# A vision tower on one core: local attention with scores on half the rows, scaling on GpSimd, one maximum and one copy per chunk, and the output product inside the loop

## What is computed

```python
h = tokens(x) @ W
h = h + L0_attn(layernorm(h))      # local attention, 16 query heads, one key/value head
h = h + L0_ffn(layernorm(h))       # 8 experts, top 2
h = h + L1_attn(layernorm(h))      # full attention, then batch norm
h = h + L1_ffn(layernorm(h))       # 8 experts, top 1 with capacity
```

```python
mask = (cols <= rows) & (rows - cols <= 128)
scores = einsum('bqgtd,bqgsd->bqgts', q, k) / 8
p = softmax(where(mask, scores, -1e30))
out = einsum(p, v) @ wo.T
```

## Time and profile before

| what | value |
|---|---|
| median of 3 runs | 1309.26 us (1307.86 to 1312.95) |
| the profiled execution | 1307.1 us, of which the span of the trace is 1305.3 us |
| PE busy | 901.9 us, 69% of the span |
| DVE busy | 834.4 us, 64% |
| ACT busy | 481.7 us, 37% |
| POOL busy | 159.6 us, 12% |
| mean granted clock of TensorE | 0.861 of full speed |
| windowed, second image | 374.8 to 499.6 us |
| its PE, DVE, ACT, POOL busy, 374.8 to 491.0 us | 105.75, 91.08, 80.25, 0.00 us |

### The profile page before, as it was taken

One profiled execution on the slowest core, in us unless ns is written; L12 is line 12 of the kernel. 1 busy time (PEld: TensorE's weight loads), 2 busy tenths in 40 slices (PEclk: granted clock), 3 DMA queues, 4 the chain that ended last, 5 costly groups with the idle time before them and its releaser, 6 DMA issues. The chain is left out here.

```text
span 1305.3 us, 18986 instructions
## 1 busy us (share of the span) xinstructions
PE 901.9 (69%) x6390; PEld 564.4 (43%) x6398; DVE 834.4 (64%) x2339; ACT 481.7 (37%) x1687; POOL 159.6 (12%) x116
## 2 busy tenths in 40 slices
PE   4477997775879986766699867766999679320630
PEld 4133664454336654453266534622666347120530
DVE  1387886754778867546788756467988465560235
ACT  0024774142237751321377622312777223000100
POOL 0051000000420000003300000024000000007145
PEclk9888999897879997887899978978999789755775
DMA  7033000000330000002400000014100000300112
GB/s 242 11 62 130 2 2 1 1 1 3 60 132 2 2 2 1 1 3 44 148 2 2 2 1 0 3 27 119 46 2 1 1 1 1 98 1 26 62 47 43
DMA packets 51381, 43.40 MB, mean 33 GB/s; under 512 B 46452, under 2 KB 47892, under 8 KB 50356
## 3 DMA queue, kind: packets, MB, share of 16 engines
q1 hardware_dynamic: 49222, 39.91, 10.5%
q0 software_dynamic: 2048, 2.10, 0.7%
HBM read 29.21 MB, written 4.72 MB: 26 GB/s over the span
## 5 line engine op out<-in xcount | busy, mean ns | idle before, releaser
L696 ACT ACTIVATE work<-ps,small,rq 128x160 f32<-128x160 f32 x512 | 241.3, 481 | 134.5 <-DVE small L659 134.5
L593 PE MATMUL ps<-kT,big 128*128 128x320 f32 x512 | 185.6, 469 | 0.0
L654 DVE TENSOR_REDUCE small<-ps 128x2 f32<-128x320 f32 x256 | 113.7, 486 | 50.3 <-PE ps L593 48.1
L260 PE MATMUL ps<-xT,s_proj_w 64*128 64x512 f32 x384 | 126.6, 794 | 26.1 <-DVE xb L533 13.8
L668 DVE TENSOR_SCALAR work<-work,small 128x128 f32<-128x128 f32 x512 | 112.0, 282 | 4.5
L624 PE MATMUL ps<-turned,vwin 128*64 128x128 f32 x1024 | 84.2, 283 | 27.7 <-ACT big L711 23.7
L696 ACT ACTIVATION_READ_ACCUMULATOR work<-ps,small,rq 128x1 f32 x512 | 101.8, 199 | 0.0
L593 PEld LDWEIGHTS ps<-kT,big 128*128 128x128 f32 x512 | 82.3, 199 | 24.8 <-issue 24.8
L678 DVE COPY turned<-ps 128x512 f32<-128x512 f32 x128 | 87.6, 684 | 2.4 <-PE ps L605 2.4
L260 PEld LDWEIGHTS ps<-xT,s_proj_w 64*128 64x128 f32 x384 | 46.8, 247 | 89.9 <-issue 61.3
L564 POOL TENSOR_TENSOR big<-xb 128x1024 f32<-128x1024 f32 x32 | 75.6, 2374 | 60.0 <-DVE xb L533 60.0
(11 more groups left out here) (240 smaller groups left out, 1504.1 us busy)
## 6 DMA issues: line engine op xcount, KB each, us to landing
xb<-in_x SPq DMA_DIRECT2D x5, 4096.0 KB, 13.5
vrem<-xb SPq DMA_DIRECT2D x64, 64.0 KB, 2.1
s_proj_w<-in_proj_w SPq DMA_DIRECT2D x1, 1536.0 KB, 6.2
sent_rows<-zeros SPq DMA_DIRECT2D x8, 160.0 KB, 4.0
big<-sent_rows SPq DMA_DIRECT2D x5, 256.0 KB, 3.5
answered_rows<-big SPq DMA_DIRECT2D x8, 160.0 KB, 1.8
xb<-in_ffn_w SPq DMA_DIRECT2D x1, 1028.0 KB, 5.5
out<-vrem SPq DMA_DIRECT2D x8, 128.0 KB, 2.0
```

What stands on the lines that cost most here:

```text
L260: ins = nc.tensor.matmul(bank[banks + w][:], proj_w[half_rows(w), cols], xT[half_rows(w), :], start=True, stop=True)
L593: ins = nc.tensor.matmul(tiles, qT[:, c, 4 * hh:4 * hh + 4, :].rearrange("p a t -> p (a t)"), kT[:, :, CHUNK * c:CHUNK * c + SPAN], start= ...
L654: ins = v.tensor_reduce(small[:, c % 4, 0, 2 * e:2 * e + 2], s_bank(c, e)[:, 0:2 * SPAN].rearrange("p (a k) -> p a k", a=2), X, ALU.max)
L696: nc.scalar.activation(probs[:, c % 3, q, :], s_bank(c, q // 2)[:, SPAN * (q % 2):SPAN * (q % 2) + SPAN], ACT.Exp, bias=small[:, c % 4, 1, ...
```

## The change

Seven things are changed together in `windowed`, with what they need in `setup` and `project`:

1. `kT` holds the keys once. The scores of `e` = 0 use partitions 0 to 63 and those of `e` = 1 partitions 64 to 127: four matmuls of 160 columns on half the rows in place of two of 320 on all rows, and the mask matmuls likewise (two per chunk, as before). `e` = 0 and `e` = 1 go to different banks. The groups are ordered q = 2e + hh in place of 2hh + e.
2. One `TENSOR_REDUCE` of 640 columns over both banks, which writes its four maxima to PSUM (`row_max`).
3. The scaling moves from DVE to POOL: two `TENSOR_TENSOR`, of 512 and of 128 columns. DVE keeps the reciprocal and signals `sums_inverted`.
4. The transposes go to bank 4 and the start of bank 5, one set in place of two; one copy of 640 columns by DVE takes both to `pT`, and ACT's `pTr` copy goes away.
5. The values' outputs move from the scores' banks to banks 6 and 7, one set; ACT takes both with one copy of 256 columns, which signals `oT_ready`. `values` is done one step earlier: PE's step n is `scores(n)`, `turn(n-2)`, `values(n-3)`. The `oT` copy of ACT stays at n-4, behind the exponentials of n. `values(c)` now waits for `oT_ready` to reach c, which is the copy of chunk c-1.
6. The output product is made per tile of 128 tokens, 8 matmuls of 64 columns each: seven tiles inside the loop, in `turn` of every fourth chunk from chunk 7 on, and the last after it. DVE adds each to `h` in `add_out`. The product at the end, ACT's copy of it and its transposes go away.
7. `project` writes `kT` with one instruction. `setup` loads the mask and the row selector twice, once per half of the partitions.

```diff
-                        for e in range(2):
-                            r = half_rows(e)
-                            ins = v.scalar_tensor_tensor(out=kT[r, e, WINDOW:], in0=k_turned[r, :], scalar=wqk[r, 0:1],
-                                                         in1=ps[r, 6:8, :].rearrange("p a n -> p (a n)"), op0=ALU.mult,
-                                                         op1=ALU.mult)
-                        ins.then_inc(S["v_dve"], 1)
+                        v.scalar_tensor_tensor(out=kT[:, WINDOW:], in0=k_turned, scalar=wqk[:, 0:1], in1=both_banks(6),
+                                               op0=ALU.mult, op1=ALU.mult).then_inc(S["v_dve"], 1)
...
+                    for hh in range(2):
+                        for e in range(2):
+                            ins = nc.tensor.matmul(tiles[e][:, hh, :],
+                                                   qT[half_rows(e), c, 4 * hh:4 * hh + 4, :].rearrange("p a t -> p (a t)"),
+                                                   kT[half_rows(e), CHUNK * c:CHUNK * c + SPAN], start=False, stop=True,
+                                                   skip_group_check=True)
...
+                def out_product(i):
+                    pe.wait_ge(S["oT_ready"], NQ * (i + 1))
+                    for p in range(PAIRS):
+                        ins = nc.tensor.matmul(wo_at(i), oT[:, p, P * i:P * i + P], sbuf["wo0"][:, p, :], start=(p == 0),
+                                               stop=(p == PAIRS - 1), skip_group_check=True)
...
                 def turn(c):
                     pe.wait_ge(S["scaled"], c + 1)
-                    if c >= 2:
-                        pe.wait_ge(S["pT_ready"], c - 1)
-                        pe.wait_ge(S["pTr_ready"], c - 1)
+                    if c >= 1:
+                        pe.wait_ge(S["pT_ready"], c)
+                    if added(c):
+                        out_product((c - 7) // 4)
...
                 def values(c):
                     pe.wait_ge(S["pT_ready"], c + 1)
-                    pe.wait_ge(S["pTr_ready"], c + 1)
-                    if c >= 2:
-                        pe.wait_ge(S["oT_ready"], c - 1)
-                    pe.wait_ge(S["exp_done"], NQ * min(c + 3, CHUNKS))
+                    if c >= 1:
+                        pe.wait_ge(S["oT_ready"], c)
...
-                                o = s_bank(c, hh)[D * e:D * e + D, 2 * SPAN:2 * SPAN + P]
+                                o = bank[6 + hh][half_rows(e), 0:P]
...
-                for n in range(CHUNKS + 4):
-                    if n >= 4:
-                        values(n - 4)
+                for n in range(CHUNKS + 3):
                     if n < CHUNKS:
                         scores(n)
                     if 2 <= n < CHUNKS + 2:
                         turn(n - 2)
-                pe.wait_ge(S["oT_ready"], CHUNKS)
...
+                    if n >= 3:
+                        values(n - 3)
+                out_product(TILES - 1).then_inc(S["wo_done"], 1)
                 turn_normed(pe, 1)
...
+                        ch.step(v.tensor_reduce(row_max(c),
+                                                ps[:, s_banks(c), 0:2 * SPAN].rearrange("p e (h k) -> p e h k", h=2), X,
+                                                ALU.max))
...
+                        if added(c):
+                            add_out((c - 7) // 4)
+                        v.tensor_copy(pT[:, c % 2, :],
+                                      ps[:, 4:6, :].rearrange("p a n -> p (a n)")[:, 0:(NQ + 1) * P]).then_inc(
+                                          S["pT_ready"], 1)
...
+            @block.gpsimd
+            def _(g):
+                for c in range(CHUNKS):
+                    g.wait_ge(S["sums_inverted"], c + 1)
+                    if c >= 2:
+                        g.wait_ge(S["transposed"], c - 1)
+                    g.tensor_tensor(probs[:, c % 3, :, 0:P], probs[:, c % 3, :, 0:P], bc(small[:, c % 4, 3, :], P),
+                                    ALU.mult)
+                    g.tensor_tensor(own[:, c % 2, :].rearrange("p (q k) -> p q k", q=NQ), probs[:, c % 3, :, P:SPAN],
+                                    bc(small[:, c % 4, 3, :], CHUNK), ALU.mult).then_inc(S["scaled"], 1)
...
                     c = n - 4
                     if c >= 0:
                         a.wait_ge(S["pv_done"], c + 1)
-                        for hh in range(2):
-                            ins = nc.scalar.activation(
-                                oT[:, 4 * hh:4 * hh + 4, CHUNK * c:CHUNK * (c + 1)],
-                                s_bank(c, hh)[:, 2 * SPAN:2 * SPAN + P].rearrange("p (a t) -> p a t", t=CHUNK),
-                                ACT.Copy)
-                        ins.then_inc(S["oT_ready"], 1)
-                a.wait_ge(S["proj_done"], 1)
-                nc.scalar.activation(tokensT, bank[0][:], ACT.Copy).then_inc(S["v_act"], 1)
+                        nc.scalar.activation(
+                            oT[:, :, CHUNK * c:CHUNK * (c + 1)].rearrange("p (h a) t -> p h a t", h=2),
+                            ps[:, 6:8, 0:P].rearrange("p h (a t) -> p h a t", t=CHUNK),
+                            ACT.Copy).then_inc(S["oT_ready"], 1)
```

More of the change, by code:

```diff
@@ L179, in program @@
         pTr_own = sb("pTr_own", [P, 4, P])
-        pTr, own = pTr_own[:, 0:2, :], pTr_own[:, 2:4, :]
+        own = pTr_own[:, 2:4, :]
         sums_turned = pTr_own[:].rearrange("p a n -> p (a n)")
@@ L298, in _ @@
                     r = slice(D * half, D * half + D)
+                    for dst, src in ((row_of_t_rows, "row_of_t"), (window_mask_rows, "window_mask")):
+                        sp.dma_start(dst[D * half:D * half + CHUNK], inp[src]).then_inc(first_sem, 16)
+                        n += 1
                     for dst, src in ((qn, "q_norm"), (kn, "k_norm"), (bq, "bq1"), (bk, "bk1")):
@@ L334, in _ @@
                 v.tensor_tensor(both_halves[:], ident[:, 0:D], ident[:, D:P], ALU.add)
-                v.tensor_copy(row_of_t[0:CHUNK], sbuf["row_of_t"])
-                v.tensor_copy(window_mask[0:CHUNK], sbuf["window_mask"])
+                for half in range(2):
+                    r = slice(D * half, D * half + CHUNK)
+                    v.tensor_copy(row_of_t[r], row_of_t_rows[r])
+                    v.tensor_copy(window_mask[r], window_mask_rows[r])
                 ch.step(v.tensor_scalar(wqk[:], qn[:], kn[:, 0:1], float(np.sqrt(D)), ALU.mult, ALU.mult))
@@ L567, in windowed @@
         def windowed(block, b):
-            def s_bank(c, half):
-                return bank[2 * (c % 2) + half]
             @block.sync
@@ L575, in _, with s_banks, row_max, added @@
                 sp.wait_ge(S["x_loaded"], 16)
+            def s_banks(c):
+                return slice(2 * (c % 2), 2 * (c % 2) + 2)
+            def row_max(c):
+                return ps[:, s_banks(c), HALF - 2:HALF]
+            def added(c):
+                return c % 4 == 3 and c >= 7
+            def wo_at(i):
+                return bank[5][:, HALF - D * (1 + i % 2):HALF - D * (i % 2)]
             @block.tensor
@@ L596, in scores @@
-                    ins.then_inc(S["scores_done"], 1)
+                    tiles = [bank[2 * (c % 2) + e][:, 0:2 * SPAN].rearrange("p (h k) -> p h k", h=2) for e in range(2)]
+                    for e in range(2):
+                        if c < EARLY:
+                            mask, masked = rows(window_mask[half_rows(e), variant, :], 2), tiles[e]
+                        else:
+                            mask = window_mask[half_rows(e), variant].rearrange("p (g k) -> p g k", k=CHUNK)
+                            mask = mask[:, ::SPAN // CHUNK - 1, :].unsqueeze(1).to_broadcast([D, 2, 2, CHUNK])
+                            masked = tiles[e].rearrange("p h (g k) -> p h g k", k=CHUNK)[:, :, ::SPAN // CHUNK - 1, :]
+                        nc.tensor.matmul(masked, row_of_t[half_rows(e)], mask, start=True, stop=True,
+                                         skip_group_check=True)
@@ L663, in _ @@
                         v.wait_ge(S["exp_done"], NQ * (c + 1))
-                        ch.step(v.reciprocal(small[:, c % 4, 3, :], small[:, c % 4, 2, :]))
-                        if c >= 2:
-                            v.wait_ge(S["transposed"], c - 1)
-                        for q in range(NQ):
-                            v.tensor_scalar(probs[:, c % 3, q, 0:P], probs[:, c % 3, q, 0:P], small[:, c % 4, 3, q:q + 1],
-                                            None, ALU.mult)
-                        v.tensor_tensor(own[:, c % 2, :].rearrange("p (q k) -> p q k", q=NQ), probs[:, c % 3, :, P:SPAN],
-                                        bc(small[:, c % 4, 3, :], CHUNK), ALU.mult).then_inc(S["scaled"], 1)
+                        v.reciprocal(small[:, c % 4, 3, :], small[:, c % 4, 2, :]).then_inc(S["sums_inverted"], 1)
                     c = n - 2
@@ L694, in _ @@
                             a.wait_ge(S["transposed"], c - 2)
[L695 to L706 removed]
```

(7 more changed lines are left out.)

80 lines of the change are left out of this document (23 added, 57 removed).

## The result

The changed kernel takes **1695.76 us** (median of 4 runs, 1688.53 to 1700.01), against 1308.56 for the kernel before in the same session: 1.2949 times as long (95% interval 1.2922 to 1.2977), or 387 us more. The forecast was 1600 with a range of 1535 to 1675. The direction was right, and so was the mechanism up to the clock; the size was too small by 96 us, and the result lies outside the range.

A forecast was written before the change was run, and what follows sets the result against it. PE's throughput bound the loop before; a ring through PE, DVE and ACT would bind it after. 27 x (6.1 - 3.16) less 7 is 72.4 us an image, 291 with four images and setup: 1600 us, range 1535 to 1675.

The forecast's parts named there:

- the ring: Loop: `oT` copy, behind exponentials of n, holds `values(n-3)`, and `scores(n+1)` stands behind them; 5.55 us a turn at full clock.
- six step lengths: In the ring: scores to maximum 1.00, maximum to exponential 1.05, exponentials 1.86, copy 0.38, copy to values 0.26, values 0.96 us.
- first four turns: Filling the pipe: chunk 4's scores start 10.6 us after chunk 0's, before 11.9; -1.3 us an image.
- Rivals 3 and 4: Loop: 3, the ring doesn't close, about 1253 us, chance 0.03; 4, POOL late for the transposes, 1697 us, chance 0.03.
- the price of a low clock in a turn: In the ring at 1.2 GHz: at most a doubling of scores and values, 1.8 us; turn 6.5 to 7.3, estimate 6.9.
- I expect it to go to and fro: PE's clock in the loop: alternates between 2.4 and 1.2 GHz, so a turn of 6.1 us, between 5.55 and 6.9.
- PE's busy time should hardly rise: Whole kernel: a sign of the forecast, PE's total busy time hardly rises; no size given.
- Rival 2: Loop: the same ring, always at 1.2 GHz; 1687 us as a median, chance 0.17.
- the end of the stage, -4.5 us: Behind the loop, scores of chunk 31 to DVE's sum: 14.3 us where 18.8 stood, -4.5 us an image.
- `kT` and setup: `kT` in one instruction: -1.1 us an image; setup's two more DMAs and doubled casts: +1.6 us once.
- The output product at nothing: Every fourth turn of the loop: the output product, 1.8 us, lies in PE's gap of 3.1 us in the ring.

The follow-up runs named there:

- first experiment: The changed kernel with ACT's `oT` copy of chunk n-4 moved ahead of the exponentials of chunk n: 1267.84 us, 0.9692 of the kernel before.
- the wait alone: The kernel before with one condition changed, the values of chunk c waiting for the `oT` copy of chunk c-1: 1868.56 us, one run.
- the products out of the ring: The changed kernel with all eight output products per tile, and DVE's eight sums, made behind the loop: 1700.24 us, one run.
- the kernel with the fill: The changed kernel with 12 unread bfloat16 matmuls of 384 columns in PE's gap in turns without an output product: 1522.5 us, one run.
- the scaling's 36 us: The first experiment with the scaling put back on DVE and POOL's part removed: 1303.4 us, 0.9966 of the kernel before.
- the half rows' 45: The first experiment with the scores computed again on all rows, keys stored twice with zeros: 1313.31 us, 1.0048 of the kernel before.
- the product's -21: The first experiment with the output product made once behind the loop, as in the kernel before: 1247.03 us, 0.9537 of the kernel before.

## Why the prediction was right in kind and wrong in size

**Right: the ring.** Its place (ACT's order of exponentials and copy, wanted by `values(n-3)`), its length at full clock (5.51 worked out and 5.55 taken, 5.30 measured), its idle time (2.81 us behind L722 at full clock), and that nothing else closes it. PE waited there 92 times where some 110 were forecast, since the turns with a product at 1.2 GHz have no gap left. The first experiment shows it by opening the ring, and the wait alone shows it by closing it in the old kernel. Four of the six step lengths came within 0.02 us. The other two were shorter than forecast: scores to maximum (0.88 for 1.00) and the end of the copy to the values (0.14 for 0.26). The first four turns took 10.7 us in two images (107.86 to 118.56) and 11.45 in two, 10.6 forecast. Rivals 3 and 4 fell: no turn ran near 3 us, and POOL's product takes 1.04 us and waits 638 us in all.

**Right: the price of a low clock in a turn.** The forecast was 6.9 for 5.55, 1.35 more; measured were 6.66 for 5.30, 1.36 more.

**Wrong: how often the clock is low.** The step "I expect it to go to and fro", with 6.1 between the two levels, failed. In the first and last image the loop from chunk 4 to chunk 31 took 181.5 us (118.56 to 300.07 in the first), in the other two 179.1 (482.78 to 661.89), 6.68 a turn on average. That is about the turn of 6.66: what the products add, the few turns at a higher clock take back. The forecast's reason for the mix was that the output product in the gap makes the work nearly unbroken, so that the clock should rise there. A turn with one and the turn after it:

```profile
149.50:157.50 8.00, 8.00 (x55) 6.68 (x53) 2.04 (x5) 2.25 (x9) 1.40 (x2) 0.50 0.01 2
157.90:160.90 3.00, 1.09 (x11) 0.68 (x9) 1.79 (x4) 1.49 (x7) 1.36 (x2) 1.00 0.01 3
161.40:177.40 16.00, 11.11 (x84) 7.75 (x86) 3.81 (x8) 4.75 (x19) 2.79 (x4) 0.50 0.00 0
```

PE worked all of the 8 us, at 1.2 GHz. The clock did rise behind it, during the next scores, but then came the next gap (busy 1.09 of 3 us), and it was low again when the values ran. The scores and transposes of one turn were all that had it. The unbroken stretch was not needed for such a rise either: with the products out of the ring the clock rose as often. What makes it rise there no run shows. The sign that PE's busy time should hardly rise failed too: it rose by 210 us. At 6.68 for 6.10, the loops are 62 us above the forecast in 108 turns. This hides a piece of luck. With the mix of the forecast (6.1 lies 0.41 of the way from 5.55 to 6.9) the measured levels 5.30 and 6.66 give 5.86, so the mix by itself is 89 us off, and the ring that was taken 0.25 too long gives 27 back. The Trainium skill (TensorE: Matmul & The Clock Gate, section "HAM oscillation — how this bites in real kernels") describes a loop in which every iteration starts at the low clock. Its loop waits 3 to 5 us in each iteration; here gaps of 2.81 and then 2.25 us did it, and the windows' 0.58 and 0.61 agree with the low clock. Rival 2, which has this as its mechanism, was the nearest of the cases with 1687, though it had a chance of only 0.17. Its nearness is partly luck: 24 us too much for the loops (404 for 380) stand against 39 too little for all the rest.

**Wrong: the end of the stage, -4.5 us.** From the scores of chunk 31 to DVE's sum it took 22.8 us (300.07 to 322.67 and 0.2 for the sum), where 18.8 stood before and 14.3 was forecast. The steps named in the forecast add up to 13.3 (3.9, 1.6, three times 1.8, 0.4 for the copy, 1.8 and 0.2), so 1.0 of its 14.3 has no step. Two rows of the changed kernel, and one of the kernel with the fill:

```profile
309.67 3.68 PE L615 MATMUL ps<-s_wo,big 128*128 128x64 f32 x16
...
322.67 0.22 DVE L662 TENSOR_TENSOR h<-h,ps 128x64 f32<-128x64 f32 x1 [7.26 <-PE ps L615]
```

```profile
277.04 0.22 DVE L668 TENSOR_TENSOR h<-h,ps 128x64 f32<-128x64 f32 x1 [4.14 <-PE ps L615]
```

At full clock the same end took 14.9 us (262.35 to 277.04 and 0.2). The forecast had the end at 2.4 GHz while it let the loop run between the levels; a price was set on the clock in one place and left out in the next. It also missed that the last product inside the loop has no gap to lie in, since there are no exponentials left to wait for. 8.5 us in four images is 34 us.

The two together are 96 us. The span grew by 392.4 us, and the forecast's sum was 291; the other 5 are in the first four turns, which gained 3 us in all where 5 were forecast, and in `kT` and setup, which were forecast at -3 together and left the rest of the kernel within 1 us of before. Not taken apart is what each of these two did.

**The output product at nothing** held at full clock: with the fill, the turn with a product from 188.10 to 193.41 was 5.31 us. At 1.2 GHz its 16 records take 3.5 us, more than the gap of 2.25. That turn took 7.76 us (149.45 to 157.21), the one after it 6.28, so a product cost 0.7 net of the clock that it brought, about 17 us in the 24 turns that hold one. Being in the ring it was not free, then, but moving it out saved nothing in all.

## What to carry to other kernels

When a consumer is moved a step earlier in a software pipeline, look up on every engine where its producer stands in that engine's own order: a copy that stands behind this step's work closes a ring of that length, and here moving it to the front of the loop's body gave back 428 us. Having found a ring, price it at the low clock first, and with it everything behind the loop: here a gap that recurs in every turn kept PE at 1.2 GHz for most of the loop, and work that raised the clock only just ahead of a gap bought little (a turn of 6.28 for 6.66). Then open it and cost the parts one by one (the scaling's 36 us, the half rows' 45, the product's -21): with the ring closed the product's place made no difference, 1700 against 1696, and the other two were not tried there. Cost them from the loop's own turns, since the clock of the tail can move the total by as much.

## What was not expected of the hardware

- A ring in which PE works 2.5 of 5.3 us fell to 1.2 GHz after one turn. There it worked 4.4 of 6.66 us with gaps of 2.25 us, and it came back only for a few us at a time: 0.58 to 0.61 over 181 and 179 us, and 0.58 to 0.62 with no products in the ring. With 2.1 us of unread matmuls in each gap the clock was 1.00 throughout the loop. In the old kernel with the added wait it went to and fro inside a turn (transposes 1.06, values 0.66 at 192.09).
- POOL's product of 128x512 float32 with a broadcast operand took 1.04 us, where the row of before, an addition, had 1.26 for two full operands.
- Eight half-row records of 160 columns took 0.69 us (0.17 a pair), the same on full rows 1.19.
- A 128x128 float32 weight load with 64 columns behind it went at 0.114 us a record at 2.4 GHz (1.83 us for 16, 157.21 to 159.04 in the first experiment) and 0.217 at 1.2 GHz (3.47 us for 16, 309.67 to 313.14).
